# Moving the spectrum loads and half of the inverse-table loads from GpSimd's DMA queue to SyncE's in an FFT-style long convolution

## What is computed

```python
# xn = layernorm(x), x is (2, 4096, 2048)
q = dwconv(xn @ Wq.T + bq); k = dwconv(xn @ Wk.T + bk); v = xn @ Wv.T + bv
kv = k * v                                        # (B, 2048 channels, L)
kv_f = rfft(kv, n=2 * L); kernel_f = rfft(ssm_kernel, n=2 * L)
y = irfft(kv_f * kernel_f, n=2 * L)[..., :L]
y = (y + kv * D_skip) * q
attn = y @ Wo.T + bo
ffn = gelu(round(clip(xn @ W1.T / 0.1)) * 0.1) @ W2.T
out = x + attn + ffn
```

## Time and profile before

| what | value |
|---|---|
| median of the three runs | 5622.13 us |
| the profiled execution's own time | 5558.23 us |
| its span, slowest core (core 4) | 5556.7 us |
| spans of the eight cores | 5506.7 to 5556.7 us |
| TensorE busy / weight loads / VectorE / GpSimd / ScalarE | 3466.0 / 1795.9 / 1403.0 / 654.3 / 414.3 us |

### The profile page before, as it was taken

How to read it: one execution, slowest core, us unless ns; L and a number is a source line. 1 busy time by engine, 2 the same in 40 slices (tenths; PEclk the granted TensorE clock), 3 DMA queues, 4 the chain that set the end, 5 groups by cost and what they waited for, 6 DMA issues and landing times. The chain is left out here.

```text
span 5556.7 us, 52301 instructions; the slowest of 8 cores (5506.7 to 5556.7 us)
## 1 busy us (share of the span) xinstructions
PE 3466.0 (62%) x18322; PEld 1795.9 (32%) x18560; DVE 1403.0 (25%) x2784; ACT 414.3 (7%) x791; POOL 654.3 (12%) x1212
## 2 busy tenths in 40 slices
PE   3777650899993527667477478406566666464644
PEld 1233220788883213223133133103222222121211
DVE  0111120254543210220310311400477772101011
ACT  0111110222220100000000000001011110000000
POOL 0000000011111001121211211200000001111111
PEclk9989975999996769889799799758899999898988
DMA  8887879222113427858768676341311112434343
GB/s 165 194 196 179 192 203 159 37 42 37 32 31 50 63 62 204 215 141 224 174 173 217 155 190 195 93 82 32 83 50 50 49 50 37 70 45 71 44 69 68
DMA packets 401726, 614.48 MB, mean 111 GB/s; under 512 B 228928, under 2 KB 283200, under 8 KB 371904
## 3 DMA queue, kind: packets, MB, share of 16 engines
q0 software_dynamic: 132320, 420.64, 36.4%
q1 hardware_dynamic: 269152, 190.48, 12.4%
HBM read 578.90 MB, written 138.94 MB: 129 GB/s over the span
## 5 line engine op out<-in xcount | busy, mean ns | idle before, releaser
L807 PE MATMUL ps<-p_kvg,p_tf 128*128 128x512 bf16 x3199 | 759.9, 394 | 344.9 <-DMA p_tf<-tblf_sp 169.2
L1095 PE MATMUL ps<-p_w,p_a 128*128 128x512 bf16 x2007 | 505.9, 396 | 389.3 <-DMA p_w<-w2T 271.5
L360 PE MATMUL ps<-p_ssm,p_tf 128*128 128x512 bf16 x2133 | 532.0, 411 | 262.4 <-ACT p_kb L377 168.3
L1039 PE MATMUL ps<-p_xn,p_w 128*128 128x512 bf16 x2007 | 463.8, 381 | 251.8 <-DVE p_u L1053 217.5
L807 PEld LDWEIGHTS ps<-p_kvg,p_tf 128*128 128x128 bf16 x3264 | 321.2, 101 | 783.2 <-issue 450.1
L533 PE MATMUL ps<-p_xq,p_wk 128*128 128x256 bf16 x3328 | 367.7, 274 | 192.3 <-DMA p_ckb<-ckb 192.3
L1095 PEld LDWEIGHTS ps<-p_w,p_a 128*128 128x128 bf16 x2048 | 190.1, 100 | 705.1 <-issue 536.3
L360 PEld LDWEIGHTS ps<-p_ssm,p_tf 128*128 128x128 bf16 x2176 | 223.4, 104 | 570.5 <-issue 359.2
L533 PEld LDWEIGHTS ps<-p_xq,p_wk 128*128 128x128 bf16 x3328 | 326.8, 98 | 231.5 <-issue 192.8
L533 PE MATMUL ps<-p_xq,p_wv 128*128 128x256 bf16 x3328 | 365.4, 273 | 0.0
L1039 PEld LDWEIGHTS ps<-p_xn,p_w 128*128 128x128 bf16 x2048 | 192.4, 98 | 523.2 <-issue 313.6
(11 more groups left out here) (80 smaller groups left out, 2270.6 us busy)
## 6 DMA issues: line engine op xcount, KB each, us to landing
p_tf<-tblf_sp POOLq DMA_DIRECT2D x136, 1024.0 KB, 7.4
tblf_sp<-p_tf SPq DMA_DIRECT2D x34, 1024.0 KB, 14.2
p_ti<-tbli_sp POOLq DMA_DIRECT2D x136, 256.0 KB, 3.0
p_wc<-w_lay POOLq DMA_DIRECT2D x128, 256.0 KB, 7.2
w_bf<-p_wc SPq DMA_DIRECT2D x128, 256.0 KB, 5.8
p_w<-w2T POOLq DMA_DIRECT2D x256, 128.0 KB, 3.3
p_x<-x_slab POOLq DMA_DIRECT2D x26, 1024.0 KB, 11.2
p_tf<-fwd_cos POOLq DMA_DIRECT2D x17, 1024.0 KB, 13.1
```

The lines of the kernel that those rows point to most:

```text
L360: return E.matmul(bank(b)[:, :GSZ], tf[par][:, sc * 128:(sc + 1) * 128], ssm_sb[:, sc * D + gg * GSZ:sc * D + gg * GSZ + GSZ], start=(sc = ...
L807: return E.matmul(bank(b)[:, :GSZ], tf[par][:, pc * 128:(pc + 1) * 128], kvg[kp3][:, pc * GSZ:(pc + 1) * GSZ], start=(pc == g.PC0), stop=( ...
L1039: return E.matmul(bank(b)[:, :TJ], w1c[par][:, hc * 128:(hc + 1) * 128], xn[:, hc * NOWN + tj * TJ:hc * NOWN + (tj + 1) * TJ], start=(hc = ...
L1095: return E.matmul(bank(tc)[:, :EOSZ], a[:, fc * NOWN + tc * 128: fc * NOWN + tc * 128 + 128], w2c[par][:, :], start=(fc == 0), stop=(fc == ...
```

## The change

The two loads of each block of the filter's spectrum move from the GpSimd queue to the SyncE queue, with the wait that precedes them. The inverse tables with odd index move too; those with even index stay. The code between them, with the transposes and the weight pieces, keeps its place.

```diff
-    gKH = [bld.dsem(f"p3gKH{i}", "gpsimd") for i in range(2)]
+    gKH = [bld.dsem(f"p3gKH{i}", "sync") for i in range(2)]
     TID = 4
-    gTI = [bld.dsem(f"p3gTI{i}", "gpsimd") for i in range(TID)]
+    gTI = [bld.dsem(f"p3gTI{i}", ("gpsimd", "sync")[i % 2]) for i in range(TID)]
...
             for kc in range(KC):
                 kp = kc % 2
                 if kc >= 2:
-                    bld.wait(rec, "gpsimd", "V", pw_done[kc - 2])
+                    bld.wait(rec, "sync", "V", pw_done[kc - 2])
                 elif gg >= 1:
                     last_same = KC - 1 - ((KC - 1 - kc) % 2)
-                    bld.wait(rec, "gpsimd", "V", pw_prev[last_same])
+                    bld.wait(rec, "sync", "V", pw_prev[last_same])
                 for ri in range(2):
-                    bld.dma(rec, "gpsimd", gKH[kp],
+                    bld.dma(rec, "sync", gKH[kp],
                             Kh[kp][ri][:, :], env["khat_sp"][ri, kc, gg])
...
                     par = gidx % TID
-                    eng = "gpsimd"
+                    eng = ("gpsimd", "sync")[par % 2]
                     if gidx - TID >= 0:
                         bld.wait(rec, eng, "T", inv_mm[gidx - TID])
                     v = bld.dma(rec, eng, gTI[par], ti[par][:, :],
```

## The result

The changed kernel takes 5682.08 us (median of 12 runs, lowest 5647.18); the kernel before, run beside it, 5655.35 us (median of 12, lowest 5558.23). The ratio is 1.0202, with a 95% interval of 1.0162 to 1.0242: slower, and the interval doesn't say whether by more or by less than 2%. The forecast was slower by 1.5%, with "within 2%" the likeliest; it came out at the edge of that, and the interval leaves the forecast out.

What follows compares the result with a forecast made beforehand. Bound taken: VectorE's serial pointwise part in phase 3, with TensorE idle, delays the end one for one. 5558.2 + 119.6 - 35 + 0.5 = 5643 us, +85; on the median 5622 + 85 = 5707 us, range 5635 to 5775.

Steps and rivals of the forecast that it cites:

- The spectrum loads behind the transposes: SyncE queue, phase 3: first pointwise operation 39.4, 40.0 and 40.2 us later in groups 0 to 2; sum +119.6 us.
- The short waits: VectorE's waits for spectrum loads, 36.8 us, go almost entirely as a pair's round trip falls below 3.18 us; taken as -35.
- The odd tables, cost 0: Inverse tables with odd index move to SyncE in phase 3: nothing to gain, cost 0, covered by four buffers.
- The bound that the text did give: Odd inverse tables: if the four buffers' cover were gone, one landing of about 3 us per group, 12 us.
- TensorE's first matmuls: After longer stands before the inverse, first matmuls cost between 0 and +2 us more each; +0.5 us in all.
- The base: Sum of +85 us added to the earlier runs' median, 5622 us, giving 5707; the profiled execution's 5558.2 gave 5643.
- one of the signs that the text named for a wrong forecast: Stretches of other phases differing by more than 20 us, which nothing in the prediction accounts for.
- (a): Rival: transposes not in the way of spectrum loads, only waits go; 5521 us, on the median's base 5585; chance 0.06.
- (b): Rival: the delay comes but the waits between blocks stay; 5678 us, on the median's base 5742; chance 0.17.
- (c): Rival: transposes alone on the queues take 1.10 us each; 5624 us, on the median's base 5688; chance 0.07.
- (d): Rival: loads land late behind the transposes' backlog, about 3.4 us more per group; 5653 us (5717); chance 0.08.
- The rule of the Trainium skill: Starting DMAs from several engines only saves sequencer starting time, usually small beside the transfer; by it, change worth about nothing.

Runs made afterwards that it cites:

- the run with the other half of the tables: Changed kernel, but with the even inverse tables on the SyncE queue and the odd ones on GpSimd; ratio 1.0158 (1.0120 to 1.0197).
- The dose of 16: Kernel before with spectrum loads on SyncE, 16 of the 32 transposes ahead of them and 16 behind, all inverse tables on GpSimd; ratio 1.0093 (1.0053 to 1.0133).
- the order with none ahead: Kernel before with spectrum loads on SyncE ahead of all 32 transposes, all inverse tables on GpSimd; ratio 0.9971 (0.9926 to 1.0016).

## Why the forecast was right in its mechanism and short in its size

*The spectrum loads behind the transposes.* Right. Forecast 39.4, 40.0 and 40.2 us; the waits are 40.8, 41.3 and 40.4. The bound by stores issued behind transposes (2.3 us to land) was the right row to take. Of the 2.5 us that were missed in all (a gap of 0.11 us in each wait left out), 1.3 us are the first pair's issue and landing (0.58 and 0.43 us of issue in group 0, where 0.32 each was taken). The rest is chance: the transposes start when the last weight store is out, and in groups 0 and 1 that was 3.9 and 4.2 us ahead of the moment at which VectorE could have begun, instead of 4.8 and 5.2. On core 6 of the run with the other half of the tables the wait of group 0 is 38.0 us. The dose of 16 and the order with none ahead confirm the step.

*The short waits.* Right in kind: the round trip went under a block's 3.18 us, and -36.5 of the 36.8 us of waits went. But the pointwise part got shorter by 32.4 us only, where -35 was taken. The sum took the rows' waits for lost time, and 43 gaps of 0.11 us in them are no wait. In time, delay and short waits together are +89.7 us on core 4, which is what TensorE's stands grew by (254.0 to 343.7), against a forecast of +84.6. By the means of the table, the stands account for 4 of the 15 us that the sum lacks.

*The odd tables, cost 0.* This step failed, and it is the main miss, 11 of the 15 us. It checked what the moved loads wait for, and not what the loads left behind would now overtake. It said that the next group's loads come a step earlier "which is nothing, since TensorE then still waits for VectorE at L910". That asked only whether those loads were needed sooner. What mattered is that 1.25 MB of them now start ahead of the last table and 1.25 MB more within 0.9 us behind it. It costs 1.7 to 3.8 us of wait a group, and in 15 of 24 cases a slow last step behind it, at the lower clock where it was read: 3.6 us a group by the parts' lengths, +10.8 us in all, confirmed by the halves (0.25% for the tables alone; no such wait with the spectrum loads alone, or with the other parity). The bound that the text did give, one landing a group if the cover were gone, 12 us, was about the size, by luck: it counted four groups and a landing of 3 us, where it is three groups and a landing of 8.1 us in the one shown.

*TensorE's first matmuls.* The +0.5 us was harmless, and the range of up to 2 us a stand was not needed. The 1.3 us taken for the shorter stand was one of two values in the earlier trace rows; the other, 3.57 us for the first eight matmuls after 67.44 us, gives 1.7, as the 108.73 us do. And with stands of 96 to 102 us and the tables in one queue the inverse has its old length.

*The base.* The forecast of 5707 us was made on 5622 us, the median of three runs. By the ratio, the base that goes with 5682 us is 5682 / 1.0202 = 5570 us. So the time lies in the range, 25 us under the forecast, because the base was too high by 52 us and the sum too low by 27. That nearness is luck. The forecast for executions like the profiled one, 5643 us, misses the 5678 us of the changed kernel's profiled execution by 35, but there the slowest core lost 52 us in phase 5; so one of the signs that the text named for a wrong forecast, another phase off by more than 20 us, did appear, and not by the change. The fair test is the sum against the parts: +85 against +100.

*The rivals.* (a) fell: the transposes were in the way for 41 us. (b), waits that stay, fell too: four waits instead of 43. (c): 32 transposes took 41.6 to 42.0 us with no spectrum load beside them, so they aren't quicker alone. (d) fell: the load landed 2.3 us after issue. The rule of the Trainium skill (DMA: Bandwidth & Descriptors, "Issuing engines are not separate DMA queues") is half borne out: the transfers do share the DMA engines, as table 33 shows (8.1 us to land, the engines 97% busy). But the time that starting takes on a queue was not small here: it was the largest term.

## What to carry to other kernels

Before a DMA is moved to another queue, read both queues' timelines at that place: what it will stand behind (issuing time times count, to be paid by whoever waits, less the head start), and, in the queue it leaves, what moves up and now starts ahead of it. A burst of transfers with a late deadline belongs beside the work with the most slack; to find that, price it beside each stage. And when a stall is a serial part of one engine, look first whether that part can lie beside the stage before it: here that was worth 3.1%, and the best queue order tried about 0.3%, which isn't clear of nothing.

## What the runs showed of the hardware that was not expected

- The matmuls behind the late table, after a wait of only 3.17 us, ran at a granted clock of 0.57 over 4 us (1.00 before the wait); behind 1.70 us in group 1 they took their full-speed 1.89 us. And a stand of 96.31 us had no slower restart than one of 65.05: on core 0 the first eight matmuls took 3.57 us in the changed kernel as in the one before.
- The first plain load issued by SyncE right behind transposes took it 0.52 to 0.58 us instead of 0.32. And the second load of a pair took 0.43 us in the median of its 68 issues, the first 0.32.
- A 256 KB load issued 0.7 us after a 1 MB load of another queue, with 1.5 MB more around it, landed after 8.1 us, as long as the 1 MB loads themselves took (7.8): being small gave it no precedence.
